# Layer 1 of a graph network on one core: messages scattered as three bfloat16 parts instead of one float32 operand

## The reference, cut to what matters

```
features = H[id_Xe[0]]
M_in = jnp.concatenate([features, Xe], axis=1)
Y = jax.nn.relu(M_in @ M_W.T + M_b)
Z = jax.ops.segment_sum(Y, id_Xe[1], num_segments=H.shape[0])
U_in = jnp.concatenate([H, Z], axis=1)
H_next = jax.nn.relu(U_in @ U_W.T + U_b)
```

## Time and profile before

| | us |
|---|---|
| median of 3 runs | 5229.31 (5225.77 to 5229.66) |
| the profiled execution | 5240.01 |
| its span, first to last instruction | 5238.2 |
| layer 1's loop over the 52 groups | about 4040 to 5214 in the span |

### The profile page before, as it was taken

The page is one execution under the profiler, slowest core; times in us unless marked ns, Lnnn a source line. Parts: engine busy times, 40 slices in busy tenths (PEclk is TensorE's granted clock), DMA queues, the critical chain, the costliest instruction groups (busy, mean ns, idle before and its releaser), DMA issues.

```text
span 5238.2 us, 97613 instructions
## 1 busy us (share of the span) xinstructions
PE 3526.3 (67%) x36481; PEld 2982.6 (57%) x36481; DVE 2178.1 (42%) x3991; ACT 1542.0 (29%) x3339; POOL 1562.0 (30%) x1627
## 2 busy tenths in 40 slices
PE   3456666665566656665666566656565999999998
PEld 2445554554455545554555455545454888888887
DVE  5323332333233323332233223323335777777776
ACT  3222222222222222222222222212225555555554
POOL 3443334333443344334433443344330000000000
PEclk8666666666666666666666666666677999999999
DMA  6443444344433443444334433443332444344442
GB/s 180 107 124 103 107 118 120 108 106 118 126 107 101 117 126 103 105 118 125 113 96 119 123 112 96 117 126 106 103 78 51 78 77 75 70 74 77 77 76 54
DMA packets 914064, 539.25 MB, mean 103 GB/s; under 512 B 701164, under 2 KB 868064, under 8 KB 913880
## 3 DMA queue, kind: packets, MB, share of 16 engines
q1 hardware_dynamic: 862168, 428.75, 34.9%
q0 software_dynamic: 51584, 109.05, 6.4%
q10 hardware_dynamic: 256, 0.68, 0.0%
HBM read 245.68 MB, written 292.66 MB: 103 GB/s over the span
## 4 chain that ended last, share of the span: by engine, by line
PE 42%; another core or an unknown queue 26%; issue 15%; DVE 8%; ACT 5%; DMA 1%; DVEq 1%; ACTq 1%; SPq 0%; POOL 0%; POOLq 0%
PE ps_w L805 21%; PE ps_r L792 7%; PE ps_p L767 7%; PE ps_b L777 5%; DVE arena L1157 2%; ACT arena L607 2%; DVE counted L1066 2%; DVE arena L1153 1%; PE ps_p L753 1%; PE ps_w L814 1%; ACT side L591 1%; ACT acc L580 1%; ACT dst_rel L601 1%; DVE arena L1121 1%
## 5 line engine op out<-in xcount | busy, mean ns | idle before, releaser
L805 PE MATMUL ps_w<-arena 128*64 128x128 f32 x10400 | 1751.8, 316 | 789.4 <-issue 741.1
L493 POOL DMA_INDIRECT edge_store<-side,slot_idx x1612 | 1554.2, 964 | 2337.2 <-ACT side L594 1852.2
L805 PEld LDWEIGHTS ps_w<-arena 128*64 128x64 f32 x10400 | 1367.8, 159 | 1015.2 <-issue 919.9
L1121 DVE TENSOR_SCALAR arena<-arena,iota_p 125x512 bf16<-125x512 bf16 (+1 forms) x1352 | 467.2, 349 | 1852.0 <-ACT arena L607 1088.5
L792 PE MATMUL ps_r<-tab,arena 125*128 125x64 bf16 x15600 | 802.7, 203 | 396.1 <-issue 278.5
L1157 DVE TENSOR_TENSOR arena<-ps_c,dst_rel 128x1024 f32<-128x1024 f32 (+1 forms) x728 | 806.6, 1108 | 619.2 <-PE ps_w L805 460.2
L607 ACT ACTIVATE arena<-ps_b 125x512 bf16<-125x512 f32 (+1 forms) x1352 | 747.2, 576 | 1006.8 <-remote 774.8
L792 PEld LDWEIGHTS ps_r<-tab,arena 125*128 125x128 bf16 x15600 | 647.7, 104 | 622.3 <-issue 546.6
L637 ACT ACTIVATE arena<-arena 128x512 f32<-128x512 f32 (+1 forms) x728 | 425.4, 584 | 1908.3 <-PE ps_w L805 981.4
L777 PE MATMUL ps_b<-ident_b,marks_b 128*125 128x128 bf16 x5200 | 623.6, 253 | 205.9 <-ACT dst_rel L601 186.9
L767 PE MATMUL ps_p<-w_both,side 80*128 80x128 f32 x3224 | 605.0, 337 | 189.2 <-DVE counted L1066 118.4
(11 more groups left out here) (112 smaller groups left out, 609.5 us busy)
## 6 DMA issues: line engine op xcount, KB each, us to landing
edge_store<-zeros SPq DMA_DIRECT2D x52, 3300.0 KB
arena<-edge_store SPq DMA_DIRECT2D x104, 1650.0 KB, 9.7
side<-attr SPq DMA_DIRECT2D x156, 256.0 KB
edge_store<-side,slot_idx POOLq DMA_INDIRECT x1612
side<-attr SPq DMA_DIRECT2D x52, 224.0 KB
side<-attr SPq DMA_DIRECT2D x156, 64.0 KB
acc_kept_l<-acc SPq DMA_DIRECT2D x2, 1562.5 KB, 9.6
side<-attr SPq DMA_DIRECT2D x52, 56.0 KB
```

Of the source, the lines that this page charges most:

```text
L493: pool.indirect_dma_start(out=store, in_=stage[:, c, i, :], in_offset=None, out_offset=bass.IndirectOffsetOnAxis(ap=slot_idx[:, s, t + i:t ...
L805: last = pe.matmul(ps_sum, msg[:, slot, t, :], dst_match[:, slot, t, :], start=(u == 0 and t == 0), stop=(u == NU - 1 and t == nt - 1))
L1121: dve.tensor_scalar(src_match[0:NODE_P, slot, i % 2, 0:nt * P], spread_src[0:NODE_P, slot, i % 2, 0:nt * P], iota_p[0:NODE_P, 1:2], None, ...
```

## The change

In layer 1 alone the message is kept in float32, and split exactly into three bfloat16 parts. ACT writes the relu into `parts[..., 0, :]`. A view `parts_upper` reads the upper 16 bits of each float32 word as bfloat16. POOL subtracts the upper half of part 0 from part 0, which gives part 1, and the upper half of part 1 from part 1, which gives part 2; the second subtraction waits for the first. The scatter has its operands exchanged: the one-hot, now bfloat16 (`dst_match_b`), is loaded as weights, and the 192 columns of the three upper halves move, so that the group's sum stands as window by (3 x 64) in `ps_w`. Once a group ACT copies this sum (`copy_sum`) to `group_sum`, PE turns it and adds its parts by three float32 matmuls with the identity (`turn_sum`), and ACT copies the turned sum to `window` as before, one unit later. The product of `weight` now goes to `ps_p[0]` in layer 1. Some semaphores are merged to make room; layer 0's waits stay what they were.

```diff
+        dst_match_b = cols(arena, 2 * e_cols, UNIT * WINDOW).bitcast(BF16).rearrange("p (s t w) -> p s t w", s=2, w=WINDOW)
+        parts = cols(side, 0, 2 * UNIT * PARTS * D).rearrange("p (s t k d) -> p s t k d", s=2, k=PARTS, d=D)
+        parts_upper = cols(side, 0, 2 * UNIT * PARTS * D).bitcast(BF16)\
+            .rearrange("p (s t k h) -> p s t k h", s=2, t=UNIT, h=2)[:, :, :, :, 1]
...
+            def split(m, s, u):
+
+                nt = UNITS[u][1]
+                slot = (s + u) % 2
+                pool.wait_ge(dense_sems[1].relu_done, units(m, u) + 2)
+                pool.tensor_tensor(parts[:, slot, 0:nt, 1, :], parts[:, slot, 0:nt, 0, :], parts_upper[:, slot, 0:nt, 0:D],
+                                   ALU.subtract).then_inc(rest_split, 1)
+                pool.wait_ge(rest_split, units(m, u))
+                pool.tensor_tensor(parts[:, slot, 0:nt, 2, :], parts[:, slot, 0:nt, 1, :], parts_upper[:, slot, 0:nt, D:2 * D],
+                                   ALU.subtract).then_inc(parts_done, 1)
...
+            def copy_sum(m, s):
+                act.wait_ge(dense_sems[1].scattered, units(m, NU - 1) + 2)
+                act.wait_ge(sum_turned, m + 1)
+                act.activation(group_sum[:, s, :], ps_sum[1], ACT.Copy).then_inc(sum_copied, 1)
...
-                act.activation(window[:, s, :], ps_sum, ACT.Copy).then_inc(d.window_copied, 1)
+                act.activation(window[:, s, :], (ps_sum[0], ps_turned)[layer], ACT.Copy).then_inc(d.window_copied, 1)
...
-                    if u == 2 and not first:
+                    if u == 2 and layer == 1 and not first:
+                        copy_sum(m - 1, 1 - s)
+                    if u == 2 + layer and not first:
                         copy_window(layer, m - 1, 1 - s)
...
-                    act.activation(msg[:, slot, 0:nt, :], pre[:, slot, 0:nt, :], ACT.Relu).then_inc(d.relu_done, 1)
+                    act.activation((msg[:, slot, 0:nt, :], parts[:, slot, 0:nt, 0, :])[layer], pre[:, slot, 0:nt, :], ACT.Relu)\
+                        .then_inc(d.relu_done, 1)
...
+                else:
+                    pe.wait_ge(parts_done, units(m, u))
+                    if u == 0:
+                        pe.wait_ge(sum_copied, m)
+                    for t in range(nt):
+                        last = pe.matmul(ps_sum[1], dst_match_b[:, slot, t, :], parts_upper[:, slot, t, :], **ends[t])
...
+            def turn_sum(m, s):
+
+                pe.wait_ge(sum_copied, m + 1)
+                pe.wait_ge(dense_sems[1].window_copied, m + 2)
+                for k in range(PARTS):
+                    last = pe.matmul(ps_turned, group_sum[:, s, k * D:(k + 1) * D], prm("identity"),
+                                     start=(k == 0), stop=(k == PARTS - 1))
+                last.then_inc(sum_turned, 1)
...
+                    if i == 5 and layer == 1 and not first:
+                        turn_sum(m - 1, 1 - s)
...
-                    dve.tensor_tensor(dst_match[:, slot, 0:nt, :], iota.unsqueeze(1).broadcast_to([P, nt, WINDOW]),
+                    dve.tensor_tensor((dst_match, dst_match_b)[layer][:, slot, 0:nt, :], iota.unsqueeze(1).broadcast_to([P, nt, WINDOW]),
```

More of the change, by code:

```diff
@@ L86, in __init__ @@
         self.e_landed = [own(f"e_landed_s{s}") for s in range(2)]
-        self.e_free = [own(f"e_free_s{s}") for s in range(2)]
         self.meta_done = own("meta_done")
@@ L299, in build @@
         slots_ready = sem("slots_ready")
[L300 removed]
         ranking_begun = sem("ranking_begun")
+        pool_released = sem("pool_released")
+        pe_released = sem("pe_released")
+        rest_split = sem("rest_split")
+        parts_done = sem("parts_done")
+        sum_copied = sem("sum_copied")
+        sum_turned = sem("sum_turned")
         sp_released = sem("sp_released")
@@ L526, in _ @@
                                    ALU.subtract).then_inc(centred[1], 1)
+            def split(m, s, u):
[7 more added lines that the diff above has]
+                                   ALU.subtract).then_inc(parts_done, 1)
+            with pool.Fori(0, TURNS) as n:
+                for s in range(2):
+                    for u in range(NU):
+                        split(n * 2 + s, s, u)
             if_general(pool, lambda: general(1))
@@ L640, in dense @@
                         evacuate(m + 2, s, 2 * u - 3)
+                if last and layer == 1:
+                    copy_sum(m, s)
                 if last:
@@ L799, in scatter @@
                 slot = (s + u) % 2
-                pe.wait_ge(d.relu_done, units(m, u) + 2)
+                ends = [dict(start=(u == 0 and t == 0), stop=(u == NU - 1 and t == nt - 1)) for t in range(nt)]
                 pe.wait_ge(d.dst_matched, units(m, u))
-                if u == 0:
-                    pe.wait_ge(d.window_copied, m + 2)
-                for t in range(nt):
-                    last = pe.matmul(ps_sum, msg[:, slot, t, :], dst_match[:, slot, t, :],
-                                     start=(u == 0 and t == 0), stop=(u == NU - 1 and t == nt - 1))
-                last.then_inc(d.scattered, 1)
+                if layer == 0:
+                    pe.wait_ge(d.relu_done, units(m, u) + 2)
+                    if u == 0:
+                        pe.wait_ge(d.window_copied, m + 2)
+                    for t in range(nt):
+                        last = pe.matmul(ps_sum[0], msg[:, slot, t, :], dst_match[:, slot, t, :], **ends[t])
+                else:
+                    pe.wait_ge(parts_done, units(m, u))
+                    if u == 0:
+                        pe.wait_ge(sum_copied, m)
+                    for t in range(nt):
+                        last = pe.matmul(ps_sum[1], dst_match_b[:, slot, t, :], parts_upper[:, slot, t, :], **ends[t])
+                last.then_inc(d.scattered, 1)
+            def turn_sum(m, s):
[5 more added lines that the diff above has]
+                last.then_inc(sum_turned, 1)
             def weight(layer, m, s):
@@ L812, in weight @@
                 pe.wait_ge(d.accumulated, m + 1)
-                pe.sem_inc(d.weighting_begun, 1)
-                pe.matmul(ps_post, prm(("w1_twice", "u_sum")[layer], D)[:, 0:D], window[:, s, :],
+                pe.sem_inc(pe_released, 1)
+                pe.matmul(ps_post[layer], prm(("w1_twice", "u_sum")[layer], D)[:, 0:D], window[:, s, :],
                           start=True, stop=True).then_inc(d.weighted, 1)
@@ L846, in dense @@
                         scatter(layer, m, s, u)
+                    if layer == 1:
+                        turn_sum(m, s)
                     weight(layer, m, s)
@@ L1129, in accumulate @@
                 dve.tensor_tensor(acc[:, bass.ds(start, WINDOW)], acc[:, bass.ds(start, WINDOW)],
-                                  ps_post, ALU.add).then_inc(d.accumulated, 1)
+                                  ps_post[layer], ALU.add).then_inc(d.accumulated, 1)
             def begin(layer):
```

49 lines of the change are left out of this document (24 added, 25 removed).

## The result

The changed kernel takes 5336.32 us (5334.99 to 5337.85), the kernel before 5227.54 beside it (5225.10 to 5229.66): a ratio of 1.0208 with a 95% interval of 1.0191 to 1.0226, 109 us slower. The forecast was 5386, and slower.

The account below looks back on a forecast made before the run. PE was taken to bound layer 1. Steps of 16.40 + 2.81 + 3.86 + 2.50 give a group of 25.57 us against 22.57, times 52 +156 us, forecast 5386; own range 5294 to 5449, 8-in-10 range 5120 to 5460.

Parts of the forecast that it names:

- The bound moves to the loop through ACT and DVE: Layer 1: relu, copy, matches, add, next relu take 2.71 us, above PE's 2.10 us a unit.
- A match and a subtraction shut each other out: Layer 1: a DVE match and a POOL subtraction cannot run together; a held match ends 0.25 us after the subtraction.
- Whoever waits gets in first: DVE and POOL in layer 1: when one's instruction ends, the waiting engine goes next, so second subtraction before second match.
- The size of a full step: Layer 1, relu to relu, units 0 to 4: 4.10 us each, four steps 16.40 us a group.
- The step 6-0: Layer 1, relu of unit 6 to relu of the next group's unit 0: forecast 2.50 us.
- PE's slack: Layer 1: PE has 2 us of slack, into which the 0.7 us of `turn_sum` falls.
- rival 4: PE at 1.2 GHz for stretches, about 1 us a group, 5440; or slower POOL subtractions; above 5449, chance 0.11.
- the forecast's case: Layer 1 matches and subtractions exclude each other, the waiting one goes next: group 25.57 us, 5386 us, chance 0.38.
- The scatter's price: PE in layer 1: 8 bfloat16 matmuls of 192 columns at 0.10 us, 0.78 us a unit.
- 1: Rival: DVE keeps its turn, second match before second subtraction; group 21.45 us, time 5172 us, chance 0.27.
- 2: Rival: subtractions do not exclude matches; full steps 2.71 us, group 19.03 us, time 5046 us, chance 0.12.
- 3: Rival: both orders of second match and second subtraction mixed from unit to unit; between 5172 and 5386 us, chance 0.12.

Follow-up runs that it names:

- e1: Changed kernel with both POOL subtractions cut to 2 columns of one tile; ratio 0.9679 to the kernel before, -116 us.
- e2: Kernel before, float32 scatter kept, plus the two POOL subtractions writing to a place nobody reads; ratio 1.0305 to the kernel before, +109 us.
- e5: Changed kernel with layer 1's source matches as two-tensor comparisons, second operand in PSUM; ratio 1.0076 to the kernel before, +30 us.
- e4: Changed kernel with only the second subtraction waiting for both matches; ratio 0.9800 to the kernel before, -67 us.
- e6: Changed kernel plus 12 unread matmuls on PE behind the scatters of units 0 to 3; ratio 1.0195 to the kernel before, +70 us.
- e10: e4 with turn, window copy, weight and accumulate one unit later; ratio 0.9715 to the kernel before, -102 us.
- e0: Changed kernel itself, run again as the measure for later runs; ratio 1.0292 to the kernel before, +105 us.
- e3: Changed kernel with the wait for both matches ahead of the first subtraction, so both are late; ratio 0.9900 to the kernel before, -39 us.
- e7: Changed kernel plus a third, unneeded POOL subtraction behind each pair; ratio 1.0363 to the kernel before, +133 us.
- e8: e4 plus 6 unread matmuls behind the scatters of units 0 to 3; ratio 0.9723 to the kernel before, -102 us.
- e11: e10 plus 6 unread matmuls behind the scatters of units 0 to 3; ratio 0.9688 to the kernel before, -113 us.

## Why the prediction was right, and where its terms were off

- **The bound moves to the loop through ACT and DVE.** Right. e1 gives it bare: 2.70 us in 0-1, where 2.71 was worked out.
- **A match and a subtraction shut each other out.** Right, shown by e1, e2, e5, by the 0.15 us of the held matches and the 0.895 us of the held subtractions. The step that carried it from a DMA instruction of GpSimd to a subtraction held.
- **Whoever waits gets in first.** The order came out as forecast, first match, second subtraction, second match, in 187 of 208 full steps; in the other 21, all in the step 2-3, both matches were late and came behind the second subtraction. But the reason given was not the one at work: the second subtraction does not wait there, it starts early enough, 0.01 us behind the second match where 0.048 would have been too late. That this race of hundredths went the forecast's way was luck. e4 shows what the other order is worth, 172 us.
- **The size of a full step, 4.10 us against 3.71 in the mean of four.** The mis-sized terms are two. The first subtraction starts 0.08 us after the relu's end (4501.39 against 4501.31), not 0.16; the one row used was the slowest start of its kind. And the second starts 0.08 us after the first's end, at 4502.51, while the first match runs until 4502.58, and still takes 1.04: 0.07 us is within the 0.14 that can pass beside a match, so it is not pushed behind it, as my sum had it (ready at 1.99, started at 2.08). The second match then ends 0.15 after it instead of 0.25. By these numbers, 0.71 + 1.04 + 0.08 + 1.04 + 0.15 = 3.02 for the second match's end (the sum had 3.37), and with -0.08 + 0.69 + 0.11 the step is 3.74; measured 3.73 in the step shown. Over the four full steps the excess was 1.56 us a group, in 4-5 and 5-6 another 0.47.
- **The step 6-0, 2.50 us against 3.54.** The term that failed is PE's slack. I let the copies start behind the short relu, as inside the group. But there PE has the next group's spreads, a full scatter and a gather to do before it can feed them, and at the lower clock. e6 parts it: 0.78 us comes back with the fill and the full clock in all 49 groups; the other 0.26 is that order. e1 missed by the same term, and mostly by its clock: 3.57 us in 43 groups at the low clock, 2.59 in the three at the full one.
- **The sum.** The two errors had opposite signs: -1.56 - 0.47 + 1.04 = -0.99 us a group, times 52 = -51 us, which leads from 5386 to 5335 (measured 5336). The forecast was nearer than its parts.
- **The clock** was priced at about 1 us a group in rival 4 and held for unlikely. It came, in part, on top of the forecast's case: 0.85 to 0.87 in layer 1, where PE's busy share was 0.71 and not near half. Taken into the sum alone it would have given the 5440 of rival 4, farther off; only with the full steps put right as well (3.71 us) does it lead to the measured time.
- **The scatter's price.** 0.78 us a unit of 8 tiles was worked out. In e6, where the fill follows it at once, it takes 2803.09 - 2802.40 = 0.69. A moving operand of every other bfloat16 costs nothing that shows.
- **Rivals.** 1 was what e4 makes true by a wait (worked out 5172, which is -57 us; e4 measured -67). 2 was false. 3 was not seen: the second match never came before the second subtraction.

## What to carry to other kernels

Before work is given to an idle GpSimd, look at which VectorE instructions use the quick form with all operands in SBUF, and at what moment they are due: what counts is not how busy GpSimd becomes but whether its instructions stand where a match is due on the loop that sets the step. If they do, order the two by a wait, or write the VectorE instruction with an operand in PSUM; both turned a loss of 105 us into something better here (+30 us), and the wait into a gain (-67 us). Where two engines fall due within hundredths of a microsecond, don't forecast the winner: put the order into the program. And when an engine stops being the bound, price its lower clock at the places where it is still late; its mean over the stretch says little (e10, e6).

## What the runs showed of the hardware that I had not expected

- A held match ends a fixed time after the subtraction: 0.150 us for 512 elements, 0.083 for 256.
- A held subtraction of 512 ends a fixed time after the match, 0.895 us (0.894 to 0.898 in the changed kernel, e0, e3 and e7). The longest of the changed kernel's 364 second subtractions, 1.113 us, is such a one; one that starts less than 0.14 us before the match's end takes its usual 1.04.
- Who goes first is decided by hundredths of a microsecond: the subtraction up to 0.045 us behind the match's start, the match from 0.048 on, without an exception in ten runs.
- Work that nobody reads made a kernel faster three times (e6 by 35 us, e8 by 35 against e4, e11 by 12 against e10), by the clock at which other work of PE ran.
- The same program's layer 0 ran at 114 GB/s in the first pair and at 202 on the three chips of the experiments, 1600 us of difference, with layer 1 equal to 0.01 us a step. Why is open.
